# Five attention stages on one core: another order in the DMA queue, and in the masked stage half of the score tiles over ScalarE and GpSimd

## The reference, cut to what matters

```
logits = einsum('bqhd,bkhd->bhqk', q, k) + mask      # mask: 512 x 512, an input
p = softmax(logits, axis=-1)
x = x + einsum('bhqk,bkhd->bqhd', p, v).reshape(...) @ o_w.T + o_b
```

## Time and profile before

| what | value |
|---|---|
| median of 3 runs | 4701.06 us (4698.58 to 4720.01) |
| the profiled execution | 4725.3 us |
| its span, first to last instruction | 4723.6 us |
| mean granted clock of TensorE | 0.923 |
| busy: TensorE, VectorE, ScalarE, GpSimd | 4283.3, 2568.7, 2255.5, 1317.2 us |
| stages SELF0, CROSS0, CROSS1, SELF2, CROSS2 | about 651, 533, 535, 759, 539 us |
| MLP0 with what lies around it; MLP2 and SELF3 | about 335; 1343 us |

### The profile page before, as it was taken

How to read it: one execution, slowest core, us unless ns; L and a number is a source line. 1 busy time by engine, 2 the same in 40 slices (tenths; PEclk the granted TensorE clock), 3 DMA queues, 4 the chain that set the end, 5 groups by cost and what they waited for, 6 DMA issues and landing times. The chain is left out here.

```text
span 4723.6 us, 63401 instructions
## 1 busy us (share of the span) xinstructions
PE 4283.3 (91%) x20306; PEld 2058.4 (44%) x20306; DVE 2568.7 (54%) x6513; ACT 2255.5 (48%) x4789; POOL 1317.2 (28%) x1405
## 2 busy tenths in 40 slices
PE   6888899999797899999999999999798899999998
PEld 3333333333464333333444443333266455555555
DVE  4555557776013677777777776777211344444443
ACT  2444446666221566654444446666321455555554
POOL 2222221110221011111111111111121566566664
PEclk7888789999897899999999999999699999999999
DMA  4322334443001444333222224343100000000000
GB/s 92 77 58 59 59 60 92 75 77 53 19 0 29 95 77 74 66 55 67 48 47 45 47 48 91 74 71 70 39 0 22 10 1 10 10 10 10 10 6 10
DMA packets 135466, 219.93 MB, mean 47 GB/s; under 512 B 42736, under 2 KB 45168, under 8 KB 133488
## 3 DMA queue, kind: packets, MB, share of 16 engines
q1 hardware_dynamic: 135152, 216.02, 22.7%
HBM read 59.69 MB, written 5.51 MB: 14 GB/s over the span
## 5 line engine op out<-in xcount | busy, mean ns | idle before, releaser
L937 ACT ACTIVATE Pr<-ST 128x512 f32<-128x512 f32 (+3 forms) x2560 | 1339.8, 565 | 1355.1 <-PE ST L510 930.4
L510 PE MATMUL ST<-stk 50*128 50x512 f32 (+3 forms) x2560 | 1076.3, 478 | 94.1 <-ACT Pr L937 81.0
L1132 DVE TENSOR_REDUCE mx<-MX 128x1 f32<-128x512 f32 x1056 | 702.7, 684 | 359.7 <-PE MX L510 357.7
L510 PE MATMUL MX<-stk 48*128 48x512 f32 (+3 forms) x1760 | 745.9, 464 | 162.2 <-DMA stk<-mrows 139.4
L510 PE MATMUL OV<-Pr,V 128*32 128x512 f32 (+3 forms) x5120 | 713.7, 633 | 2.5 <-ACT Pr L937 1.5
L1487 POOL TENSOR_SCALAR Pr<-Pr,mx 128x128 f32<-128x128 f32 (+3 forms) x512 | 548.4, 1083 | 384.8 <-DVE mx L1270 384.8
L510 PEld LDWEIGHTS MX<-stk 48*128 48x128 f32 x1760 | 320.3, 199 | 710.2 <-issue 353.7
L510 PEld LDWEIGHTS ST<-stk 50*128 50x128 f32 x2560 | 447.3, 199 | 313.4 <-ACT Pr L937 274.9
L1384 POOL CAST mhl<-mx 128x16 fp32r<-128x16 f32 x160 | 31.4, 196 | 1650.4 <-DVE mx L1132 1079.2
L510 PE MATMUL OV<-stk 48*128 48x512 f32 (+3 forms) x800 | 364.4, 455 | 6.1 <-DVE mx L1132 5.8
L1132 DVE TENSOR_REDUCE mx<-OV 128x1 f32<-128x512 f32 x480 | 326.5, 680 | 60.6 <-PE OV L510 60.4
(11 more groups left out here) (137 smaller groups left out, 6802.6 us busy)
## 6 DMA issues: line engine op xcount, KB each, us to landing
stk<-hi SPq DMA_DIRECT2D x640, 128.0 KB, 3.8
stk<-lo SPq DMA_DIRECT2D x320, 128.0 KB, 3.9
misc<-misc SPq DMA_DIRECT2D x160, 128.0 KB
sums<-spread SPq DMA_DIRECT2D x80, 256.0 KB
misc<-in_ctx_t SPq DMA_DIRECT2D x24, 512.0 KB, 5.2
W_even<-in_w SPq DMA_DIRECT2D x4, 1024.0 KB, 5.2
W_even<-in_w SPq DMA_DIRECT2D x2, 2048.0 KB, 10.7
XH<-in_ctx_rows SPq DMA_DIRECT2D x8, 512.0 KB, 4.3
```

The lines of the kernel that those rows point to most:

```text
L510: return nc.tensor.matmul(o, l, r, start=start, stop=stop)
L937: nc.scalar.activation(Pr[:, i % 2, h, q0:S], ST[h % 2][:, q0:S], ACT.Exp).then_inc(ex_done, 1)
L1132: nc.vector.tensor_reduce(m, bank[:, :], AX.X, ALU.max).then_inc(mx_red, 1)
```

## The change

It has two parts. In the queue's `slot`, `spread_rows` goes behind `max_rows(U, half, 1)`, and `max_rows(U + 1, 1 - half, 0)` ahead of `move(U, half, 0)`; this holds for all five attention stages. In SELF2, heads 1 and 3 of each tile (`BY_POOL`) get the mask by GpSimd: `exp_tile` copies their scores from the bank to the probability buffer, GpSimd's new `add_mask` adds `mask_k` there, in place, and ScalarE's new `late_exp` takes the exponential in place, one tile later. Head 0 of even tiles stays with VectorE (`by_vector`), head 2 and head 0 of odd tiles get the mask by products on TensorE (`by_tensor`). The probabilities of SELF2 go through three buffers instead of two (`PR`, `pr_buffer`), the third in a part of `stk` that was unused, and `values` comes two tiles after the scores instead of one (`lag`), with a wait for `late_done`; the last two tiles of a unit fall into the next slot. `product_out` and `invert` move a tile or half a tile back there.

```diff
+        Pr_third = nc.alloc_sbuf_tensor_at("Pr_third", [P, G, S], F32, offset=hot + 4 * 24 * S)
+        PR = [Pr[:, 0, :, :], Pr[:, 1, :, :], Pr_third]
...
-        MASKED_BY_PE = (1, 3)
+        BY_POOL = (1, 3)
+        def by_vector(i, h):
+            return h == 0 and i % 2 == 0
+        def by_tensor(i, h):
+            return h not in BY_POOL and not by_vector(i, h)
+        def pr_buffer(s, u, i):
+            return PR[(8 * u + i) % 3 if ATTN[s][2] else i % 2]
... the queue's slot
                     if on["tail"]:
                         move(U - 1, 1 - half, 1, GB - 1 + half)
-                        spread_rows(U - 1, 1 - half)
                     if on["b"]:
                         max_rows(U, half, 1)
                     if on["tail"]:
+                        spread_rows(U - 1, 1 - half)
                         widen(U - 1, 1 - half)
...
+                    if on["m"]:
+                        max_rows(U + 1, 1 - half, 0)
                     if on["b"]:
                         move(U, half, 0, GB)
-                    if on["m"]:
-                        max_rows(U + 1, 1 - half, 0)
... TensorE
+                            causal, lag = ATTN[s][1], 1 + ATTN[s][2]
+                            if i < tail_lag and j == tail_j and on["tail"]:
+                                values(tail_s, tail_u, U - 1, 1 - half, par if half else 1 - par, 8 - tail_lag + i)
+                            if j == (3 if causal or crossing else 1) and on["b"] and i >= lag:
+                                values(s, u, U, half, par, i - lag)
...
-                    if addmask and h in MASKED_BY_PE:
+                    if addmask and by_tensor(i, h):
... in values
+                    if addmask:
+                        pe.wait_ge(late_done, len(BY_POOL) * (8 * u + i + 1))
... ScalarE
+                            if h in BY_POOL and i > 0 and on["b"] and addmask:
+                                late_exp(s, u, i - 1, h)
...
-                            if at == ((1, 0) if causal_e else (0, 2)) and on["tail"]:
+                            if at == ((1, 0) if causal_e else (1, 2) if lagged(s, u) else (0, 2)) and on["tail"]:
                                 product_out(U - 1, 1)
...
+                    func = ACT.Copy if addmask and h in BY_POOL else ACT.Exp
+                    nc.scalar.activation(pr_buffer(s, u, i)[:, h, q0:S], ST[h % 2][:, q0:S], func).then_inc(ex_done, 1)
+                def late_exp(s, u, i, h):
+                    at = len(BY_POOL) * (8 * u + i) + BY_POOL.index(h)
+                    act.wait_ge(pool_masked, at + 1)
+                    tile = pr_buffer(s, u, i)[:, h, :]
+                    nc.scalar.activation(tile, tile, ACT.Exp).then_inc(late_done, 1)
... VectorE
-                            if on["b"] and addmask and j not in MASKED_BY_PE:
+                            if on["b"] and addmask and by_vector(i, j):
                                 add_mask(u, U, i, j)
-                            if at == (1, 3) and on["tail"]:
+                            if at == ((2, 3) if lagged(s, u) else (1, 3)) and on["tail"]:
                                 invert(U, 1 - half)
... GpSimd: add_mask(u, U, i) for i = 0 to 7 between the slot's other operations
+                def add_mask(u, U, i):
+                    for h in BY_POOL:
+                        pool.wait_ge(ex_done, 32 * U + 4 * i + h + 1)
+                        tile = pr_buffer(s, u, i)[:, h, :]
+                        nc.gpsimd.tensor_tensor(tile, tile, mask_k[:, i % 4, :], ALU.add).then_inc(pool_masked, 1)
```

More of the change, by code:

```diff
@@ L221, in waits, with lagged @@
                 wait(eng, s, v)
-        MASKED_BY_PE = (1, 3)
+        BY_POOL = (1, 3)
[3 more added lines that the diff above has]
+            return h not in BY_POOL and not by_vector(i, h)
+        def lagged(s, u):
+            return ATTN[s - 1 if u == 0 and s in JOINED else s][2]
+        def pr_buffer(s, u, i):
+            return PR[(8 * u + i) % 3 if ATTN[s][2] else i % 2]
         def brow_count(s):
@@ L558, in slot @@
                             at = (i, j)
[L559 to L563, removed]
+                            causal, lag = ATTN[s][1], 1 + ATTN[s][2]
+                            tail_s, tail_u = (s - 1, UNITS - 1) if u == 0 and s in JOINED else (s, u - 1)
+                            tail_lag, tail_j = 1 + ATTN[tail_s][2], 3 if ATTN[tail_s][1] else 1
+                            if i < tail_lag and j == tail_j and on["tail"]:
+                                values(tail_s, tail_u, U - 1, 1 - half, par if half else 1 - par, 8 - tail_lag + i)
+                            crossing = tail_lag > lag and i < tail_lag
+                            if j == (3 if causal or crossing else 1) and on["b"] and i >= lag:
+                                values(s, u, U, half, par, i - lag)
                             if at == (2, 0) and on["b"]:
@@ L648, in score_tile, with values @@
                     last.then_inc(st_full, 1)
-                def values(causal, U, half, vpar, i):
+                def values(s, u, U, half, vpar, i):
+                    _, causal, addmask = ATTN[s]
                     g, kt = i // 4, i % 4
+                    if addmask:
+                        pe.wait_ge(late_done, len(BY_POOL) * (8 * u + i + 1))
                     if kt == 0:
@@ L657, in values @@
                     for h in range(G):
-                        last = mm(OUT[32 * h:32 * h + 32, q0:S], Vh[:, vpar, kt, 8 * half + G * g + h, :], Pr[:, i % 2, h, q0:S],
+                        last = mm(OUT[32 * h:32 * h + 32, q0:S], Vh[:, vpar, kt, 8 * half + G * g + h, :], pr_buffer(s, u, i)[:, h, q0:S],
                                   kt == 0, kt == NT - 1)
@@ L905, in slot @@
                                 rows_out(U + 1, 0)
-                            if at == ((5, 0) if causal else (4, 2)) and on["b"]:
+                            if at == ((5, 0) if causal else (5, 2) if addmask else (4, 2)) and on["b"]:
                                 product_out(U, 0)
@@ L1390, in attention @@
                 n = ATTN_NO[s]
-                causal = ATTN[s][1]
+                _, causal, addmask = ATTN[s]
                 def slot(u, c, b, p, on):
@@ L1396, in slot @@
                     U, GB = UNITS * n + u, NB * n + b
+                    adds = addmask and on["b"]
                     norm = norm_of(s, u)
@@ L1406, in slot @@
                         clear(U, 0)
+                    if adds:
+                        add_mask(u, U, 0)
                     if norm is not None:
@@ L1410, in slot @@
                         clear(U, 1)
+                    if adds:
+                        add_mask(u, U, 1)
                     if norm is not None:
@@ L1414, in slot @@
                         clear(U, 2)
+                    if adds:
+                        add_mask(u, U, 2)
                     if norm is not None:
@@ L1418, in slot @@
                         clear(U, 3)
+                    if adds:
+                        add_mask(u, U, 3)
                     if on["m"]:
@@ L1422, in slot @@
                         clear(U, 4)
+                    if adds:
+                        add_mask(u, U, 4)
                     if on["tail"]:
@@ L1428, in slot @@
                         clear(U, 5)
+                    if adds:
+                        add_mask(u, U, 5)
                     if half == 1 and sums_of(s, u):
@@ L1432, in slot @@
                         clear(U, 6)
+                    if adds:
+                        add_mask(u, U, 6)
+                    if adds:
+                        add_mask(u, U, 7)
                     if u == UNITS:
```

12 lines of the change are left out of this document (7 added, 5 removed).

## The result

The changed kernel takes 4550.07 us (median of 4 runs, 4539.97 to 4564.75) against 4710.53 us before: a ratio of 0.966, 95% interval 0.9615 to 0.9707, 160 us less (the median before is of four runs here, the three of the table above and one more). The ratios of this document leave out two executions at a far lower clock, 5878 us of m_only and 16025 us of all_pe_mid. The forecast was 250 us less, 4451 us, with a range from 4395 to 4530. The direction was right, the size was not, and the time lies above the range. The profiled execution has a span of 4563.0 us, 160.6 less than before.

A forecast was written before the change was run, and what follows sets the result against it. TensorE, busy 91%, was taken as the bound, with stalls for the maxima's rows. Stalls 116, cross-stage clock 48, SELF0 clock 10 and masked stage 76 sum to 250 us: 4701.06 becomes 4451, range 4395 to 4530.

The forecast's parts named there:

- The bound and the stall: TensorE, busy 91%, waits 3.86 us for the maxima's rows in 38 even slots; 30 outside the masked stage give 116 us.
- What is late next?: At the odd-to-even change of slot no wait of the stall's size is listed, so nothing was deducted.
- cross pairs stay above 62: Sign of a wrong forecast: an even and an odd cross slot together above 62 us, where 59 was expected.
- The clock, 48 us in the cross stages: TensorE's half-clock time after stalls all goes in the cross stages: 23 x 2.1 = 48 us.
- Rival 2: Stalls go, but other gaps hold TensorE's clock low where it is: 4525 us; chance 0.08.
- SELF0, 37 us: Gain forecast for the causal stage SELF0, including 10 us for the clock, weighed between 0 and 28.
- The masked stage, 94.9 to 85.4 us a pair: SELF2, per slot pair: 4.6 chain, less 1.0 ScalarE, plus 3.86 stall and 2.0 clock; eight pairs give 76 us.
- The chain's VectorE half: Masked even tiles' first half: 2.54 us with head 0 over VectorE, against 2.31 by TensorE's own work in odd tiles.
- The clock in the masked stage: SELF2: about half of 4.1 us lost a pair follows stalls, so 2.0 a pair gained; range 0 to 4.
- rival 1: Mask's new way gains nothing, ScalarE being late in strict order: 4480 us, or 4504 with 3 a pair lost; chance 0.22.
- 3: Rival 3: TensorE's bare work is reached, a masked pair at 76 us, eight giving 151: 4376 us; chance 0.05.
- Rival 5: Another thing ready only at the slot's end holds the next slot by as much; only the mask's 29 remain: 4672; chance 0.05.

The follow-up runs named there:

- m_only: Changed kernel with the old queue order, so the mask's new way alone against the kernel before: ratio 1.001 (0.9986 to 1.004).
- all_pe_mid: all_pe with `move` of the second group put between the key and query transfers of `stack`, as in move_mid: 4444.52 us, ratio 0.943 to the kernel before.
- inv_late: Changed kernel with VectorE's `invert` at step (2, 3) in every stage instead of only SELF2: 4468.65 us, ratio 0.947 to the kernel before.
- move_mid: Changed kernel with `move` of the second group between the key and query transfers of `stack`, not behind all six: 4472.57 us, ratio 0.948 to the kernel before.
- q_only: Kernel before with the new queue order alone, mask as before: 4591.02 us, ratio 0.973 (0.969 to 0.977).
- late_short: inv_late with ScalarE's late exponential cut to 32 of 512 columns: ratio 0.945 (0.941 to 0.949) to the kernel before.
- pool_short: inv_late with GpSimd's mask additions cut to the first 128 of 512 columns: ratio 0.946 (0.942 to 0.950) to the kernel before.
- all_pe: inv_late with head 0 of even tiles masked by products on TensorE, VectorE adding none: 4432.65 us, ratio 0.940 to the kernel before.

## Why the prediction was wrong, point by point

- *The bound and the stall.* Right: 38 waits for `stk<-mrows` before, none after; even cross slots fell from 35.0 to 31.1 us, the 3.86 us that were forecast.
- *"`move` still goes at 2414.35, the transfers behind it (`stack`) too, so nothing behind is later. ... What is late next? ... I take nothing."* This is the step that failed. In absolute time nothing in the queue is later, but the slot begins 3.8 us sooner, so relative to the slot what stands behind `op_full` is later: in the two slots above, `move` (at 843.81 before) by 3.9 us, the end of the six `stack` transfers by 3.1, and behind them `move` of the second group by 1.6, on which `invert` waits with the maxima behind it. I looked for the next wait at the other change of slot, where no queue had been moved, and for what a moved transfer does to its own user, not for what the *unmoved* ones do once the stall before them is gone. Part of the stall's 3.9 us came back, as 1.7 us of waiting on TensorE, an odd slot of 30.8 us for 28.7, and the low clock after it. As an estimate, 23 odd slots of 2.1 us are 48, and the 78 us that the clock is low beyond inv_late's, at the 0.44 by which CROSS2's 33.8 exceed 30.8, are 34: together the missing 81. inv_late and move_mid show it: without that wait the cross stages gain 137 us, the sum's figure. The prediction's own sign, "cross pairs stay above 62", came true in CROSS2 (64.7 us), and not in most of CROSS0 (61.8).
- *The clock, 48 us in the cross stages.* The size was right: it is inside those 137, at a clock of 1.00. In the changed kernel two thirds of it stayed (TensorE is at the low level for 134 us of the three cross stages before, 94 after, 16 in inv_late), since the new wait brings the low level on as the old one did; in CROSS2 the share is 0.95 before and after. Rival 2, that it stays low through other gaps, was in that sense the rival that came nearest: 4525 us. I had given it 0.08, and priced it without a wait of its own.
- *SELF0, 37 us.* It gained 33; with `invert` late 55. There too the new wait took its share (1.8 to 2.4 us on TensorE in six of its odd slots), and the 10 us taken for the clock were low: 55 less the stalls' 27 is 28, the upper end of what was weighed.
- *The masked stage, 94.9 to 85.4 us a pair.* 85.0 at the full clock, 71 us in the stage for 76. SELF2 has no such wait, and not for its `invert` at (2, 3): q_only has it at (1, 3) there and VectorE waits in none of its masked slots either. Its own terms: q_only's slots of 44.6 and 43.9 become 43.0 and 42.0, 3.5 us a pair for 4.6 - 1.0 = 3.6. ScalarE (0.7 for 1.0, late_short) and GpSimd (nothing, pool_short) were about as charged; the addition took 1.28 for 1.27, the late exponential 0.64 where one from a bank takes 0.60. The chain's VectorE half was worth 0.7 us a pair for 1.8 (all_pe). The chain's slots were too short as well, a pair of 82.7 before and 79.1 after against 88.5 (q_only) and 85.0, by 5.8 and 5.9 us: the error is the same on both sides and drops out of the gain. That the gain came out to 0.1 us is in part luck, as terms within it were off.
- *The clock in the masked stage* I took for a constant gain. It depends on the kernel as a whole: with the faster cross stages it falls in the middle of four even slots (inv_late) where it fell in two (the changed kernel), and for 3.4 us in the last slots alone in all_pe.
- *The range* took in rival 1 and the near part of 2 and 3, each with the stalls' gain whole, and missed by 20 us. Rival 5 asked for another thing that is late, but only for one that holds the next slot by as much; it looked at the `stack` transfers issued by 2396.5 and not at the six that are issued when the slot begins. No rival joined a stall that goes with a smaller one that comes.

## What to carry to other kernels

A stall is cover for every transfer that is issued during it. Before counting its whole length as gain, take the queue's entries behind it, move the next slot forward by the stall's length, and look for the first instruction that waits for one of them in order, with others queued behind it. And where TensorE is near its full clock, compare kernels by slots at the same clock first: an edit's own microseconds can be hidden, or brought, by a fall of the clock somewhere else in the slot.

## What the runs showed of the hardware that was not expected

A 128x512 addition in float32 takes GpSimd 1.28 us with two different tiles and 1.04 us when both operands are the same tile; with 128 columns it takes 0.46. ScalarE's exponential of such a tile takes 0.64 us from on-chip memory and 0.60 from a bank. A transfer of 8 KB landed 4.7 us after its issue behind seven of 128 KB, where the maxima's 16 KB with nothing ahead but one `move` (128 KB and 8 KB) took 2.5. And the masked stage of inv_late lost 3.5 us in each of four even slots, in which TensorE is at 1.2 GHz for 10.2 us from 27 us into the slot (46.7 us instead of 43.2), though it stood idle no longer in them (1.5 us, in waits of up to 0.65) than in those at 2.4 GHz; with eight mask products more per slot (all_pe) no such wait is left, and it is at 2.4 GHz nearly throughout.
